# Normalised x and the attention output turned by transposing DMAs in 16-bit planes instead of by TensorE

## What is computed

```python
x = x + ln(attn(ln(x)))            # 16 heads of 32, q, k, v = ln(x) @ W_qkv, rotary q and k,
                                   # mask (j <= i) & (j >= i - 128), out @ W_out + b_out
x = x + ln(ffn(ln(x)))             # w = ternary(W); silu(x @ w_up.T) * (x @ w_gate.T) @ w_down.T
# ternary(W) = clip(round(W / s), -1, 1) * s,  s = mean(|W|) + 1e-8
```

## Time and profile before

| | |
|---|---|
| median of 3 runs (range) | 1361.12 us (1360.89 to 1362.19) |
| the profiled execution | 1364.31 us, of which span 1362.5 us |
| granted TensorE clock, mean | 0.989 |
| busy: PE, DVE, ACT, POOL | 1310.0, 902.5, 772.4, 696.0 us |
| one round of 32 slots, i = 3 to 6 | 157.69 us each |
| DMA queue of the kernel's transfers | 56.2% of 16 engines' span |

### The profile page before, as it was taken

How to read it: one execution, slowest core, us unless ns; L and a number is a source line. 1 busy time by engine, 2 the same in 40 slices (tenths; PEclk the granted TensorE clock), 3 DMA queues, 4 the chain that set the end, 5 groups by cost and what they waited for, 6 DMA issues and landing times.

```text
span 1362.5 us, 28292 instructions
## 1 busy us (share of the span) xinstructions
PE 1310.0 (96%) x10094; PEld 926.7 (68%) x10094; DVE 902.5 (66%) x2379; ACT 772.4 (57%) x1460; POOL 696.0 (51%) x952
## 2 busy tenths in 40 slices
PE   6688989999999999999999999999999999999997
PEld 3465755776777676777767766776767767767775
DVE  5677867777677676777667766776667676634333
ACT  3598867646555565656555556555645546633332
POOL 3354786636455365645557365554656354425432
PEclk9899988999999999999999999999999999999999
DMA  7787856663867558583667547574675737411000
GB/s 247 244 271 222 250 183 162 124 129 74 160 131 148 104 121 157 116 165 75 153 135 144 118 99 157 120 164 84 140 127 106 155 78 147 92 32 32 20 13 32
DMA packets 346589, 178.18 MB, mean 131 GB/s; under 512 B 268112, under 2 KB 321744, under 8 KB 346448
## 3 DMA queue, kind: packets, MB, share of 16 engines
q1 hardware_dynamic: 345872, 174.26, 56.2%
q10 hardware_dynamic: 576, 2.10, 0.4%
HBM read 84.48 MB, written 25.17 MB: 80 GB/s over the span
## 4 chain that ended last, share of the span: by engine, by line
PE 87%; DVE 4%; issue 2%; DMA 2%; ACT 2%; POOL 2%; SPq 1%; POOLq 0%; DVEq 0%; ACTq 0%
PE J L1370 28%; PE Y L1387 15%; PE J L1313 14%; PE J L1321 7%; PE J L1304 7%; PE S L1370 4%; PE O L1288 4%; PE S L1256 3%; PE J L1335 2%; PE Y L1264 1%; DMA spill<-split 1%; DVE turned L1059 1%; DVE prob L1049 1%; DMA parts<-in_w_up 0%; PE S L1252 0%
## 5 line engine op out<-in xcount | busy, mean ns | idle before, releaser
L1387 PE MATMUL Y<-down_q,room 128*128 128x512 fp8e4 x1024 | 262.2, 379 | 0.6 <-DVE room L1117 0.6
L1313 PE MATMUL J<-xnT,W 128*128 128x512 f32 x512 | 247.5, 612 | 2.4 <-ACT xnT L804 1.6
L820 ACT ACTIVATE prob<-prob,peak 128x256 f32<-128x256 f32 x512 | 230.1, 499 | 18.0 <-DVE peak L1049 17.9
L1049 DVE CUSTOM_DVE_ANT_0 prob<-S,band,neg_score_scale 128x256 f32<-128x256 f32 x512 | 225.8, 479 | 19.3 <-PE S L1253 12.2
L1370 PE MATMUL J<-xT,gate_q 128*128 128x256 f16 x1760 | 210.2, 273 | 4.3 <-DVE room L1103 4.3
L1370 PE MATMUL J<-xT,up_q 128*128 128x256 f16 x1776 | 212.0, 273 | 0.7 <-DVE room L1111 0.7
L1370 PEld LDWEIGHTS J<-xT,gate_q 128*128 128x128 fp8e4 x1760 | 171.2, 98 | 49.5 <-DVE room L1103 9.7
L693 POOL TENSOR_TENSOR o_n<-o_raw,rinv 128x128 f32<-128x128 f32 x128 | 53.6, 419 | 295.8 <-DVE rinv L1078 295.8
L1370 PEld LDWEIGHTS J<-xT,up_q 128*128 128x128 fp8e4 x1776 | 173.4, 98 | 44.6 <-DVE room L1111 2.1
L873 ACT ACTIVATE room<-J,sig_scale 128x512 f32<-128x512 f32 x111 | 76.0, 684 | 220.1 <-PE J L1370 220.0
L1103 DVE SCALAR_TENSOR_TENSOR room<-room,J 128x512 f32<-128x512 f32 x111 | 76.1, 686 | 169.6 <-ACT room L873 169.4
(11 more groups left out here) (143 smaller groups left out, 1983.3 us busy)
## 6 DMA issues: line engine op xcount, KB each, us to landing
spill<-split SPq DMA_DIRECT2D x64, 256.0 KB, 2.5
Qp<-spill SPq DMA_DIRECT2D x128, 128.0 KB, 2.9
Kp<-spill SPq DMA_DIRECT2D x128, 128.0 KB, 3.1
x_in<-in_x SPq DMA_DIRECT2D x32, 256.0 KB, 3.4
X<-in_x SPq DMA_DIRECT2D x32, 256.0 KB, 3.1
out_x<-X SPq DMA_DIRECT2D x32, 256.0 KB, 3.0
room<-in_w_gate SPq DMA_DIRECT2D x12, 512.0 KB, 8.3
room<-in_w_down SPq DMA_DIRECT2D x10, 512.0 KB, 5.8
```

Of the source, the lines that this page charges most:

```text
L820: e = nc.scalar.activation(prob[:, U % PROBS, a, :], prob[:, U % PROBS, a, :], ACT.Exp, bias=peak[:, U % PROBS, a:a + 1], scale=-1.0)
L1049: e = nc.vector.tensor_tensor_reduce(out=prob[:, U % PROBS, a, :], in0=S_ps[U % 2][:, a * 2 * P:(a + 1) * 2 * P], in1=mask[:], scale=neg_s ...
L1313: e = pe.matmul(dst[:], W[:, part, c, g * P:(g + 1) * P], xnT[:, c, :], start=(c == 0), stop=(c == DC - 1))
L1387: e = pe.matmul(Y_ps[t][:], h[:, q % HELD, part, (a * HT + t) * P:(a * HT + t + 1) * P], down_q[:, 2 * pair + a, :], start=(pair == 0 and ...
```

## The change

From tile 3 on, a block of normalised x no longer goes through PE, and from tile 1 on neither does a head group of the attention output. In their place:

- `split_words` (ACT): the 128x512 float32 words are read as 16-bit numbers and written as two planes (low halves, high halves) of 128x512 into `planes`, 1024 elements per partition. `planes` is the fourth buffer of `prob`; so from unit 60 on the probabilities have three buffers.
- `turn_planes` (SP): one transposing DMA of 128x1024 of 16 bit, back onto `x_in` or `o_n`, in the slot after the split and ahead of `turn(s)`.
- `merge_words`: the halves are joined to float32 words in `xnT` or `oT`; DVE does x blocks 0 and 2 and all of `oT`, ACT does x blocks 1 and 3.
- Scales: `w_scale` now goes into `rstd_x` (one more small operation on POOL), `o_scale` into the operation that takes Y from PSUM.
- Order: from i = 2 on `LATER_FILLER` replaces `FILLER`: no `T` and `OT`; Q 3 moves from slots 12, 13 to 6, 7, the Y jobs from 6 to 9, 15 to 17, 24, 25 to 8 to 11, 16, 17, 19, 20, K 3 from 13 to 15 to 12, 13, V 2 from 10, 11 to 14, 15; V 0 takes one chunk in each of slots 28 to 31. SP's spill and pack of Q 3 and K 3 move with them. ACT's `layer_norm` of x stands a slot earlier. `ff_statistics` stands in `first - 13` and `first - 10` (before: `- 13`, `- 12`), `rstd_of_half` in `first - 9` (before `- 10`), `first` being the first slot of the half.

```diff
-PROBS, PARTS, TURNED = 4, 2, 4
+PARTS, TURNED = 2, 4
+FEWER_PROBS = 60
+T_BY_DMA, OT_BY_DMA = 3, 1
...
+LATER_FILLER = [
...
+    [("Q", 3, (0, 1))],
+    [("Q", 3, (2, 3))],
+
+    [("Y", 0, (0, 1))],
+    [("Y", 0, (2, 3))],
...
+SPLIT_X = [11, 13, 15, 17]
+MERGE_X = [19, 19, 20, 20]
+SPLIT_O = [28, 30, 32, 36]
+MERGE_O = [30, 32, 34, 38]
...
+        def may_merge(engine, job):
+
+            kind, g, tile = job
+            engine.wait_ge(planes_turned, 16 * (SPLIT_NUMBER[job] + 1))
+            if kind == "T":
+                engine.wait_ge(job_full, NUMBER[("V", NG - 1, tile - 1)] + 1)
+            else:
+                engine.wait_ge(job_full, NUMBER[("Y", TT - 1, tile - 1)] + 1)
...
+            def turn_planes(job):
+
+                sp.wait_ge(split_done, SPLIT_NUMBER[job] + 1)
+                sp.dma_start_transpose(out=words(job).bitcast(U16).rearrange("p (b q) -> p b q", q=P),
+                                       in_=planes.bitcast(U16)).then_inc(planes_turned, 16)
...
+            later = {16: [], 10: [(spill_q, 3, 0)], 15: [(pack_q, 3, 0)], 17: [(spill_k, 3, 0)], 18: [(pack_k, 3, 0)],
+                     19: [], 30: [(spill_q, 1, 1)]}
...
+                for job in planes_at(s - 1, SPLIT_X, SPLIT_O):
+                    turn_planes(job)
                 if BY_PE <= s < ALL_UNITS:
                     turn(s)
...
+            def split_words(job):
...
+                if number:
+                    act.wait_ge(planes_turned, 16 * number)
+                else:
+                    act.wait_ge(p_lo_done, FEWER_PROBS)
+                nc.scalar.activation(planes.bitcast(U16).rearrange("p (s n) -> p s n", s=2),
+                                     words(job).bitcast(U16).rearrange("p (n s) -> p s n", s=2),
+                                     ACT.Copy).then_inc(split_done, 1)
...
-                if 11 <= u < 11 + TT and i + 1 < NM and s >= EARLY:
-                    layer_norm(i + 1, u - 11)
+                if 10 <= u < 10 + TT and i + 1 < NM and s >= EARLY:
+                    layer_norm(i + 1, u - 10)
...
+            def merge_words(job):
+
+                may_merge(dve, job)
+                out, halves = merge(job)
+                nc.vector.tensor_copy(out, halves).then_inc(x_merged if job[0] == "T" else o_merged, 1)
...
-                        if s == first - 13 + t:
+                        if s == first - 13 + 3 * t:
                             ff_statistics(half * HT + t)
...
-                    if s == first - 10:
+                    if s == first - 9:
                         rstd_of_half(half)
```

More of the change, by code:

```diff
@@ L144, in pieces_at, with turned_by_dma, planes_at, prob_home @@
         return []
-    table = FILLER if i else FIRST_FILLER
+    table = FIRST_FILLER if i == 0 else FILLER if i == 1 else LATER_FILLER
     pieces = [(kind, idx, tile_of(kind, idx, i), chunks) for kind, idx, chunks in table[u]]
     sums = [("M", SUM_SLOTS[s], 0, ())] if s in SUM_SLOTS else []
+    pieces = [p for p in pieces if not turned_by_dma(p[0], p[2])]
     return sums + [p for p in pieces if 0 <= p[2] < NM and not (i == 0 and (p[2] < 0 or p[:3] in PREPARED))]
+def turned_by_dma(kind, tile):
+    return kind == "T" and tile >= T_BY_DMA or kind == "OT" and tile >= OT_BY_DMA
+def planes_at(s, slots_x, slots_o):
+    i, u = divmod(s, UNITS)
+    x = [("T", t, i + 1) for t in range(TT) if u == slots_x[t]]
+    o = [("OT", g, tile) for tile in range(NM) for g in range(NG) if s == tile * UNITS + slots_o[g]]
+    return [job for job in x + o if job[2] < NM and turned_by_dma(job[0], job[2])]
+def prob_home(U):
+    return U % 4 if U < FEWER_PROBS else U % 3
+def prob_prior(U):
+    return max((V for V in range(max(0, U - 4), U) if prob_home(V) == prob_home(U)), default=None)
 PREPARED = [(kind, idx, 0) for kind, idx in BEFORE]
@@ L175 @@
     PRIOR.append(max((m for m in range(_n) if BANK[m] == BANK[_n]), default=None))
+SPLITS = [job for s in range(END) for job in planes_at(s, SPLIT_X, SPLIT_O)]
+SPLIT_NUMBER = {job: n for n, job in enumerate(SPLITS)}
 def ff_first_slot(half):
@@ L431, in load_x @@
             def load_x(tile, t):
-                at_least(sp, job_full, NUMBER[("T", t, tile - 1)] + 1 if tile else 0)
+                if tile:
+                    used(sp, ("T", t, tile - 1))
                 sp.dma_start(x_in[:, t, :], x_rows[:, tile * TT + t, :]).then_inc(x_loaded[t], 16)
@@ L556, in _ @@
                 i, u = divmod(s, UNITS)
+                for job in planes_at(s - 1, SPLIT_X, SPLIT_O):
+                    turn_planes(job)
                 if BY_PE <= s < ALL_UNITS:
                     turn(s)
-                for move, g, ahead in moves.get(u, ()):
+                for move, g, ahead in later[u] if i >= 2 and u in later else moves.get(u, ()):
                     if i + ahead < NM and s >= 2:
@@ L795, in empty @@
                     act.wait_ge(job_full, number + 1)
-                    nc.scalar.activation(oT[:, g, :], bank[:], ACT.Identity, scale=o_scale[:]).then_inc(oT_done, 1)
+                    nc.scalar.activation(oT[:, g, :], bank[:], ACT.Copy).then_inc(oT_done, 1)
                 elif kind == "T":
@@ L805, in empty @@
                                              scale=w_scale[:]).then_inc(xnT_done, 1)
+            def split_words(job):
+                kind, g, tile = job
+                number = SPLIT_NUMBER[job]
+                if kind == "T":
+                    act.wait_ge(xn_done, tile * TT + g + 1)
+                else:
+                    act.wait_ge(o_norm, (tile * NG + g + 1) * TT)
+                if number:
+                    act.wait_ge(planes_turned, 16 * number)
+                else:
+                    act.wait_ge(p_lo_done, FEWER_PROBS)
[3 more added lines that the diff above has]
+            def merge_words(job):
+                may_merge(act, job)
+                out, halves = merge(job)
+                nc.scalar.activation(out, halves, ACT.Copy).then_inc(x_merged_act, 1)
             def rotated_high(job):
@@ L819, in exp @@
                 for a in range(2):
[L820 to L821 removed]
+                    e = nc.scalar.activation(prob[:, prob_home(U), a, :], prob[:, prob_home(U), a, :], ACT.Exp,
+                                             bias=peak[:, prob_home(U), a:a + 1], scale=-1.0)
                 e.then_inc(exp_done, 1)
@@ L1201, in _ @@
                     p_low(U)
+                for job in planes_at(s, MERGE_X, MERGE_O):
+                    if job[0] == "OT" or job[1] % 2 == 0:
+                        merge_words(job)
                 if s % 2 == 0 and 0 <= s - LAG - 1 < ALL_UNITS:
```

107 lines of the change are left out of this document (91 added, 16 removed).

## The result

The changed kernel takes **1355.11 us** (median of 5 runs, 1353.92 to 1358.56), the kernel before 1361.86 us beside it (5 runs, 1360.89 to 1363.68). The ratio is 0.9944, 95% interval 0.993 to 0.9959: about 6.8 us, half a per cent, faster.

What follows compares the result with a forecast made beforehand. PE, busy throughout rounds 3 to 6, was taken as the bound. Terms: -19.3 (transposes off PE) + 2.0 (merges) + 11.6 (residual) = -5.7 us, from 1361.1 to 1355.4 us; range 1343 to 1364.

Steps and rivals of the forecast that it cites:

- PE bounds the rounds, and what leaves it leaves the time: Rounds 3 to 6, where PE waits for nothing: transposes leaving PE gain 19.3 us, 18.3 plus 1.0 in round 7.
- the job's price: One T or OT transpose job on PE: 0.435 us in slots not at the floor.
- the part on round 7: U of slot 18 to G of slot 31: about 2.0 us remain to gain, 1.0 taken, allowing for DVE's merges.
- the stall of slot 23: Round 7: a 1.44 us DVE wait for the FFN input's transposing DMA, its cause expected to stay.
- Merges cost 2.0 us in slots 28 to 31: DVE's merge in slot 30 makes `gated` late: 0.4 us per round for i = 2 to 6, ends 0 and 5.
- The residual behind K 3: POOL's slot 13: Y 0's residual behind K 3's rotary delays `st_f`, `hidden`, U of slot 14; 1.94 us, six rounds, 11.6.
- Splits, transfers, the rest: ACT splits 1.05 us each, transposing DMAs 3.2 us to landing, small POOL work, three `prob` buffers: all cost 0.
- (a): Rival, chance 0.15: slot 14's stall doesn't arise or is under 0.5 us; 1343.8 us, with half of it 1349.
- (b): Rival, chance 0.10: merges at half rate, 2.2 us, delay slots 20 and 30; 13.5 us instead of 2.0, so 1366.9.
- (c): Rival, chance 0.15: planes' DMAs make `p_high` late enough for PE in the four short slots; 1362.4 us, no change.
- (d): Rival, chance 0.03: a plane's transfer outlasts two slots to the next split; 1.6 us for each of 48 splits, 1432 us.

Runs made afterwards that it cites:

- `both_first`: Changed kernel with GpSimd doing the residual and the feed-forward's reciprocal roots ahead of the rotary in their slots: 1341.09 us, 0.984 of the kernel before.
- `before_twice`: Kernel before with every job of four fp32 transposes on TensorE (64 jobs) done twice: 1382.8 us, ratio 1.0132.
- `merge_twice`: `both_first` with each of the 38 merges on DVE done twice in succession: 1341.66 us against 1341.09.
- `residual_first`: Changed kernel with GpSimd doing the residual before the low halves and the rotary in every slot: 1344.58 us, 0.9865 of the kernel before.

## Why the prediction was right, and where it was not

Forecast 1355.4 us, measured 1355.11, within the range of 1343 to 1364 and on the side held likeliest. That the sum came out so well is luck in good part: it had 2.0 us for merges that cost nothing and 1.6 us too much for the residual, and it lacked 3.2 us for a stall that I had not seen. So too with a middle round, 156.57 us where I expected 156.5: it holds 1.67 + 0.63 us of stalls, not 1.94 + 0.4.

**PE bounds the rounds, and what leaves it leaves the time.** Right. -19.3 us was predicted. `both_first`, in which no stall is left, is from slot 58 on 19.7 us shorter than the kernel before, and `before_twice` gives the job's price as 0.436 against 0.435. In detail the part on round 7 was undersized: of the 3.4 us between the U of slot 18 and the G of slot 31 I counted 1.0 and held the rest back for the stall of slot 23 and for merges. But the stall went with the new table (slot 23 takes 3.41 us in `both_first`), and the stretch became 2.8 us shorter; the slots behind round 7 give back 1.2 of it.

**Merges cost 2.0 us in slots 28 to 31.** Wrong, they cost nothing. The changed kernel's G of slot 29, U of slot 30 and G of slot 31 in round i = 4, then the U of slot 0, which follows two chunks of Q again:

```profile
708.29 1.91 PE L1550 MATMUL J<-xT,gate_q 128*128 128x256 f16 x16
...
712.31 1.91 PE L1550 MATMUL J<-xT,up_q 128*128 128x256 f16 x16
...
716.33 1.91 PE L1550 MATMUL J<-xT,gate_q 128*128 128x256 f16 x16
...
721.12 1.15 PE L1550 MATMUL J<-xT,up_q 128*128 128x256 f16 x9
```

Slots 30 and 31 take 4.02 us each, slot 0 4.79, all without a bracket. I had taken 0.8 us for a merge, and there it takes 0.69. But the step that failed is the lateness that I laid out from a chain of DVE's durations, 0.55 us with a merge of 1.2: in `merge_twice`, with two merges of 0.69 us in a row, these slots are no longer. The estimate of 0.7 us that I worked out from the Trainium skill, "VectorE: DVE Perf Modes", section "The perf-mode tier table", fits the median of 0.69. I cited the table loosely, though: its 1.23 us for 2048 elements, two a cycle, stand there for float32, and its 16-bit copy has four a cycle (693 ns), by which a merge would, as an estimate, take 0.43 us. The measured merge, which doesn't read its 16-bit words in the order in which they lie, fits the two.

**The residual behind K 3.** Right in mechanism and place, a little over in size: 1.67 us, not 1.94, in each of six rounds, 10.0 instead of 11.6. POOL's part was exact: the residual ends 789.24 - 779.48 = 9.76 us after the U of slot 12, as 796.35 - 786.59 in the earlier trace rows. DVE was 0.14 us quicker from there to the end of `hidden`, and slot 14 is 0.13 us longer of itself than the 4.79 that I subtracted.

**What was missing.** `rstd_of_half` in slot 1: 0.63 us in rounds 3 to 7, 3.2 us. The diff has the move from -10 to -9 in a single line, and I costed only the DMAs and merges that come with the tables. The step that failed is that a moved step was put at nothing, without a look at the queue it joins. POOL's slot 1 has a rotary ahead of it and an addition, and slot 0 has an addition but no rotary. The 0.76 us that POOL loses there beside DVE weren't in the reckoning either.

**Splits, transfers, the rest.** Right: splits 1.05 us as taken, landing 3.4 us (3 to 4 predicted), the waits of `p_high` for transfers fell from 23.9 to 8.7 us, and none reaches PE.

**Rivals.** (a) fell, the stall is there; with 1344 us `residual_first` is nearly what (a) promised. (b) needed merges of 1.7 us or more. Some have that length, but not in slots 20 and 30, and `merge_twice` shows that even 1.4 us there cost 0.2 us a round (2.2 us were not tried). Its 13.5 us also counted six rounds where my main sum had five; with five it would be 11.3. (c) fell with the waits of `p_high`. (d) fell with the landing of 3.4 us.

Of the sum: -19.7 (PE) + 10.0 (residual) + 3.2 (`rstd_of_half`) - 0.5 (the slots behind round 7, which give back 0.7 us here and 1.2 in `both_first`) = -7.0 us, against -6.8 in the profiles from slot 58 on.

## What to carry to other kernels

- Where an engine is busy for a whole round, price the work by the pitch between its fixed points. But count only the copies that lie in such rounds.
- When a table is reordered, list for each moved step what stands ahead of it on its engine in the new slot, the helpers' small steps too. Two such steps took back 13 of 20 us, and putting them first in their slot brought these back.
- A cheap test of such a chain is to make the same order in the kernel that lacks the change: if it stalls there too, the change's own work is cleared. Here that was done for the residual only, not for `rstd_of_half`.

## What the hardware showed that I had not expected

A DVE copy of 1024 16-bit elements, in which both sides lie in SBUF, takes 0.69 us alone and 1.75 us where a POOL operation on two tensors of 512 float32 began shortly ahead of it; it then ends 0.54 to 0.56 us after that operation. Of 38 merges in the changed kernel six are of that length. POOL's operation takes 1.71 to 1.78 us instead of 1.27 only where a DVE operation that reads two tensors from SBUF (`p_low`, or the one that makes `xs`) is under way as it begins, or, in `merge_twice`, a merge. In all ten profiles no addition or residual begins so and keeps its 1.27 us, and none is long without it.

Of the DVE operations that occur with and without POOL's in the rounds of `both_first`, two alone show it: this copy and `p_low` (0.69 us alone, a median of 0.93 and at most 1.65 where POOL is busy for more than half of it). Those that read PSUM, and the statistics with one SBUF input, keep their length beside POOL (0.69 and 0.66 us). The Trainium skill says this in "GPSIMD Engine Reference", section "1. Specifications": the SBUF interfaces are shared with VectorE, with contention for DVE instructions in a two-port mode or with two SBUF inputs. The traces agree as to which operations are affected; in which mode the copy runs, no run shows. I had costed the merges without it.
